# Fifteen products of zeros at the start instead of seven, and two early row loads into another buffer

## The reference

```python
rkv = einsum('blh,hu->blu', inputs, W_rkv) + b_rkv
r, k, v = split(rkv, 3);  r = sigmoid(r);  k = exp(k);  kv = k * v
u1, u2 = scan(y[t] = lam * y[t-1] + (kv, k)[t])
x = (u1 + gamma * kv) / (u2 + gamma * k + 1e-06) * r
x = layernorm(inputs + x @ W_o + b_o)
xr = mu_r * x + (1 - mu_r) * x_prev;  xk = mu_k * x + (1 - mu_k) * x_prev
out = layernorm(x + sigmoid(xr @ W_r.T) * (square(relu(xk @ W_k.T)) @ W_v.T))
```

## Time and profile before

| | before |
|---|---|
| median of 3 runs | 2542.32 us (2540.78 to 2545.28) |
| profiled execution, its own time | 2542.95 us |
| its span (first to last event in the trace) | 2541.2 us |
| PE busy | 2509.6 us, 99% of the span |
| DVE busy | 2099.5 us, 83% |
| ACT busy | 1270.9 us, 50% |
| POOL busy | 1252.2 us, 49% |
| moved by DMA | 110.73 MB |

### The profile page before, as it was taken

One profiled execution on the slowest core, in us unless ns is written; L12 is line 12 of the kernel. 1 busy time (PEld: TensorE's weight loads), 2 busy tenths in 40 slices (PEclk: granted clock), 3 DMA queues, 4 the chain that ended last, 5 costly groups with the idle time before them and its releaser, 6 DMA issues.

```text
span 2541.2 us, 32904 instructions
## 1 busy us (share of the span) xinstructions
PE 2509.6 (99%) x11255; PEld 2075.1 (82%) x11255; DVE 2099.5 (83%) x2693; ACT 1270.9 (50%) x2157; POOL 1252.2 (49%) x1130
## 2 busy tenths in 40 slices
PE   8999999999999999999999999999999999999998
PEld 6788888878888788888888878888888878888877
DVE  8888888878888788887888888888888888888884
ACT  5544455544455354554545544455444555444555
POOL 5744445444454445545455444544444454545544
PEclk9999999999999999999999999999999999999999
DMA  4001101111011110101111111101111111110100
GB/s 178 17 34 50 51 34 36 44 39 51 34 45 39 35 51 34 50 34 35 50 46 38 34 35 50 50 34 34 35 50 50 34 39 31 49 51 34 49 27 34
DMA packets 57791, 110.73 MB, mean 44 GB/s; under 512 B 7041, under 2 KB 7041, under 8 KB 57089
## 3 DMA queue, kind: packets, MB, share of 16 engines
q1 hardware_dynamic: 56736, 108.03, 12.3%
q10 hardware_dynamic: 864, 0.28, 0.1%
HBM read 74.73 MB, written 33.55 MB: 43 GB/s over the span
## 4 chain that ended last, share of the span: by engine, by line
PE 94%; issue 2%; POOL 2%; DVE 1%; ACT 0%; DMA 0%; POOLq 0%; DVEq 0%
PE bankB L1193 13%; PE bankB L1194 13%; PE bankB L1195 13%; PE bankA L1173 13%; PE bankA L1172 13%; PE bankA L1174 13%; PE bankB L1240 4%; PE bankB L1242 4%; PE bankB L1241 4%; PE bankB L1218 2%; POOL xk_lo L449 0%; DVE att_f L939 0%; POOL wk_lo L412 0%; DMA wrkv_f<-in_w_rkv 0%; POOL att_f L422 0%
## 5 line engine op out<-in xcount | busy, mean ns | idle before, releaser
L1173 PE MATMUL bankA<-x_lo,wrkv_hi 128*128 128x512 f32 x1488 | 580.3, 390 | 14.5 <-issue 14.5
L1172 PE MATMUL bankA<-x_hi,wrkv_hi 128*128 128x512 f32 x1488 | 584.3, 393 | 3.5 <-POOL x_lo L417 3.5
L1174 PE MATMUL bankA<-x_hi,wrkv_lo 128*128 128x512 f32 x1488 | 580.4, 390 | 0.0
L923 DVE RECIPROCAL gate<-gate 128x512 f32<-128x512 f32 x128 | 429.2, 3353 | 4.4
L422 POOL TENSOR_TENSOR att_f<-att_f,gate 128x512 f32<-128x512 f32 x128 | 207.1, 1618 | 276.0 <-DVE att_f L944 276.0
L1174 PEld LDWEIGHTS bankA<-x_hi,wrkv_lo 128*128 128x128 f32 x1488 | 280.0, 188 | 74.1 <-issue 15.7
L1172 PEld LDWEIGHTS bankA<-x_hi,wrkv_hi 128*128 128x128 f32 x1488 | 280.2, 188 | 62.3 <-POOL x_lo L417 3.9
L1173 PEld LDWEIGHTS bankA<-x_lo,wrkv_hi 128*128 128x128 f32 x1488 | 280.2, 188 | 57.6 <-issue 0.5
L449 POOL TENSOR_TENSOR xk_lo<-xk_f,xk_hi 128x512 fp32r<-128x512 f32 x124 | 178.8, 1477 | 241.2 <-ACT xk_hi L707 241.2
L699 ACT ACTIVATE z<-z,shift,rstd 128x512 f32<-128x512 f32 x124 | 94.3, 808 | 356.7 <-POOL shift L442 356.7
L920 DVE SCALAR_TENSOR_TENSOR gate<-u,gate 128x512 f32<-128x512 f32 x128 | 182.9, 1429 | 104.2 <-ACT gate L647 101.8
(11 more groups left out here) (160 smaller groups left out, 5607.6 us busy)
## 6 DMA issues: line engine op xcount, KB each, us to landing
y<-in_x SPq DMA_DIRECT2D x128, 256.0 KB, 2.7
x_f<-in_xT SPq DMA_DIRECT2D x124, 256.0 KB, 4.0
out<-z SPq DMA_DIRECT2D x124, 256.0 KB, 2.1
wrkv_f<-in_w_rkv SPq DMA_DIRECT2D x3, 768.0 KB, 9.2
xk_f<-in_xT SPq DMA_DIRECT2D x4, 256.0 KB, 5.6
wo_f<-in_w_o SPq DMA_DIRECT2D x1, 1024.0 KB, 12.4
wr_f<-in_w_r SPq DMA_DIRECT2D x1, 1024.0 KB, 14.9
wv_f<-in_w_v SPq DMA_DIRECT2D x1, 1024.0 KB, 16.7
```

Of the source, the lines that this page charges most:

```text
L923: dve.reciprocal(gate[:, c % 2], gate[:, c % 2]).then_inc(rec_made, 1)
L1172: pe.matmul(bank[:], w_hi, hi[:, h], start=(h == 0), stop=False)
L1173: pe.matmul(bank[:], w_hi, lo[:, h], start=False, stop=False)
L1174: last = pe.matmul(bank[:], w_lo, hi[:, h], start=False, stop=(h == NC - 1))
```

## The change

WARM becomes 15, so `write_columns` issues fifteen products of zeros in place of seven. Block 0's rows for its third and fourth tile are loaded into `t`, in SP's `first_block`, right behind the rows of the first and second tile in `y`, without a wait and with semaphores of their own (`y_first_loaded`). `begin_sum` of block 0 reads them from there. Step 1 has two `load_rows` fewer.

```diff
--- before.py
+++ after.py
@@ -87,7 +87,7 @@
 SLOTS = [(name, first + i) for name, first, n in OTHERS for i in range(n)]
 NBANK = 4
 EXACT = (3,)
-WARM = 7
+WARM = 15
 
 KEY, VALUE, GATE = range(3)
 ORDER = (KEY, GATE, VALUE)
@@ -236,6 +236,7 @@
         x_first = [sem(f"x_first{c}") for c in range(NC)]
         x_loaded = [sem(f"x_loaded{c}") for c in range(NC)]
         y_loaded = [sem(f"y_loaded{i}") for i in range(HT)]
+        y_first_loaded = [sem(f"y_first_loaded{i}") for i in range(HT)]
         stored = [sem(f"stored{i}") for i in range(NT)]
 
         x_hi_made, x_lo_made, x_first_lo = sem("x_hi_made"), sem("x_lo_made"), sem("x_first_lo")
@@ -341,8 +342,12 @@
                 for i in range(HT):
                     tile = HT * half + i
 
-                    wait(sp, sum_begun, s.count(NT, tile - 1))
-                    sp.dma_start(y[:, i], x_rows[s.block() * NT + tile]).then_inc(y_loaded[i], 16)
+                    if not s.first():
+                        sp.wait_ge(sum_begun, s.count(NT, tile - 1))
+                    if s.first() and half:
+                        sp.dma_start(t[:, i], x_rows[tile]).then_inc(y_first_loaded[i], 16)
+                    else:
+                        sp.dma_start(y[:, i], x_rows[s.block() * NT + tile]).then_inc(y_loaded[i], 16)
 
             def load_xT(s):
 
@@ -359,10 +364,12 @@
                 load_weight(W_V)
                 load_weight(W_K)
                 load_rows(s, 0)
+                load_rows(s, 1)
 
             def step(s):
                 s1, s2 = (s.back(1), s.back(2))
-                load_rows(s1, 1)
+                if not s1.first():
+                    load_rows(s1, 1)
                 if s2.exists():
                     store(s2, 1)
                 load_rows(s, 0)
@@ -957,13 +964,17 @@
 
             def begin_sum(s, half):
                 for tile in range(HT * half, HT * half + HT):
-                    dve.wait_ge(y_loaded[tile % HT], s.count(32, 16 * (tile // HT) + 16))
+                    if s.first():
+                        dve.wait_ge((y_loaded, y_first_loaded)[tile // HT][tile % HT], 16)
+                    else:
+                        dve.wait_ge(y_loaded[tile % HT], s.count(32, 16 * (tile // HT)))
                     if s.first() and tile == 0:
                         dve.wait_ge(s_bo, 16)
                     bank_free(dve, s, "WO", tile)
                     if s.first():
                         dve.wait_ge(columns_written, WARM)
-                    dve.tensor_tensor(psum_of(s, "WO", tile)[:], y[:, tile % HT], bo[:], ALU.add).then_inc(sum_begun, 1)
+                    rows = t if s.first() and tile >= HT else y
+                    dve.tensor_tensor(psum_of(s, "WO", tile)[:], rows[:, tile % HT], bo[:], ALU.add).then_inc(sum_begun, 1)
 
             def sum_rows(s, tile):
                 return psum_of(s, "WO", tile)[:]
```

## The result

The changed kernel takes 2523.26 us (median of 6 runs, 2522.33 to 2524.09); the kernel before, timed beside it, 2544.0 us (6 runs, 2540.78 to 2545.56). The ratio is 0.992, 95% interval 0.9907 to 0.9933: 20.7 us less. The profiled execution took 2522.33 us, its span 2520.5 us against 2541.2.

What follows compares the result with a forecast made beforehand. PE's own work (94% of the chain) and the loop turns were taken to bound the kernel; 2542.95 us - 2.2 (early clock) + 0 (loads) = 2540.75, set against the median as 2540.2 us, range 2537.0 to 2543.6 us.

Steps and rivals of the forecast that it cites:

- The first term: Kernel start: fifteen products of zeros raise PE's clock early, so eleven product intervals shrink from 0.427 to 0.227 us, 2.2 us.
- The loads into `t`: DVE's four adds: 0.85 us passes, then is given back by the fourth statistics; taken as 0, bounds -0.85 and +0.7 us.
- The step that failed: PE's six loop-turn waits, 14.5 us, taken as fixed; nothing worth more than the gain in the first 100 us.
- The rival on the turns: PE's loop: eight added products move PE's code, turns get dearer, 2.3 us lost, 2544.6 or 2542.5 us; chance 0.08.
- A term of the range: Behind PE's wait for `x_lo` at 50.84 us: the half-clock stretch varies by 1 us between executions, widening the range.

Runs made afterwards that it cites:

- e1_w15: The kernel before with fifteen products of zeros in place of seven and nothing else: 2523.58 us against 2544.8, ratio 0.9918.
- e2_t_only: The changed kernel with seven products of zeros, so the loads into `t` alone: 2543.97 us against 2544.8, ratio 0.9998.
- e3_pad16: The kernel before with sixteen PE instructions that do nothing behind its seven products of zeros: 2525.42 us, ratio 0.9925.
- e7_drop4: The kernel before without four products of block 0's keys, eight PE instructions fewer ahead of the loop: 2536.75 us, ratio 0.9971.
- e6_pad6: The kernel before with six empty PE instructions behind its seven products of zeros: 2525.27 us, ratio 0.9927.
- e8_drop16: The kernel before without sixteen products of block 0's keys, 32 PE instructions fewer ahead of the loop: 2524.22 us, ratio 0.9923.
- e4_back: The changed kernel without eight products of block 0's keys, so as many instructions ahead of the loop as before: 2539.52 us, ratio 0.9981.
- e5_pad3: The kernel before with three empty PE instructions behind its seven products of zeros: 2546.98 us, ratio 1.0015.

## Why the prediction was wrong

**The first term was right.** "Eleven intervals shrink from 0.427 to 0.227 us, 2.2 us": 2.13 to 2.15 us at every point of the chain named, from ACT's key to the product at 48.71 us. PE's wait for `x_lo` kept its length (3.46 and 3.49 us), and eight products at 0.43 us follow it where seven did. The fifteen products ended at 7.01 us, within the 6.5 to 7.3 us given. The first real product started at 8.10 us, 0.2 us later than before; the prediction had it unmoved. From there to the key it took 3.05 us in place of 5.39 us, 2.3 us less, so two small errors cancel. ACT took the next weights at 11.83 us without a wait for them, near the 11.7 us given.

**The loads into `t` were rightly put at 0**, but not for the reason given. The prediction let DVE win 0.85 us and lose it again at the statistics. DVE won nothing. The adds after the change, then in e1_w15, where the rows still come into `y`:

```profile
53.12 2.39 DVE L977 TENSOR_TENSOR bankB<-y,bo 128x512 f32<-128x512 f32 x2
55.43 3.49 DVE L977 TENSOR_TENSOR bankB<-t,bo 128x512 f32<-128x512 f32 x2
```

```profile
56.36 0.72 DVE L966 TENSOR_TENSOR bankB<-y,bo 128x512 f32<-128x512 f32 x1 [0.99 <-DMA y<-in_x]
57.97 0.82 DVE L966 TENSOR_TENSOR bankB<-y,bo 128x512 f32<-128x512 f32 x1 [0.88 <-DMA y<-in_x]
...
58.71 2.31 DVE L911 TENSOR_TENSOR_SCAN u<-lam,carry,key 128x512 f32<-128x512 f32 x1
```

With the rows there, the third and fourth add take 3.49 us in place of 1.54 us, and the scan behind them starts at 58.83 us against 58.71. The first add had begun 0.13 us later as well (53.12 against 52.99 us). The two loads into `t` landed 15.9 us after their issue at 15.7 and 16.2 us, far ahead of these adds. The waits for the transfers have turned into longer adds: each of the two now starts while POOL is in a subtraction and takes 1.79 and 1.78 us, where an add alone takes 0.7 us. POOL in the changed kernel:

```profile
54.91 1.74 POOL L419 TENSOR_TENSOR wo_lo<-wo_f,wo_hi 128x512 fp32r<-128x512 f32 x1
56.63 1.74 POOL L419 TENSOR_TENSOR wr_lo<-wr_f,wr_hi 128x512 fp32r<-128x512 f32 x1
```

The third add starts at 55.43 us and the fourth at 57.13 us, each 0.5 us behind one of these, and each ends some 0.6 us after it. That the subtractions hold the adds up is read from these places in time; no run tried it by itself.

The 1.0 us between 51 and 100 us looks like a gain of the loads, since e2_t_only has it too. The loads are not needed for it: e3_pad16, which has the rows in `y`, shows it as well. POOL's `rstd` in e1_w15, against DVE's scan of the same moment:

```profile
71.94 1.63 POOL L438 TENSOR_TENSOR rstd<-ve,half_pow 128x2 f32<-128x2 f32 x1
...
71.80 1.26 DVE L939 TENSOR_TENSOR_SCAN att_f<-lam,carry,kv 128x512 f32<-128x512 f32 x1
```

and in e3_pad16:

```profile
74.40 0.70 POOL L438 TENSOR_TENSOR rstd<-ve,half_pow 128x2 f32<-128x2 f32 x1
...
74.47 1.25 DVE L939 TENSOR_TENSOR_SCAN att_f<-lam,carry,kv 128x512 f32<-128x512 f32 x1
```

Where POOL starts 0.07 us ahead of the scan it takes 0.70 us; where it starts 0.14 us behind, 1.63 us. The kernel before had 1.70 us (0.06 us behind), the changed one 0.71 us (0.10 us ahead). Of the twelve traces one more, e7_drop4, has it behind the scan (0.17 us, 1.63 us); in the other nine it starts 0.05 to 0.10 us ahead of the scan or more than a microsecond away from it, and takes 0.70 or 0.71 us. `z`, the transposes and the keys follow from it. From the product behind the wait for `x_lo` to the 192nd behind it, past the keys' waits, PE takes 46.3 us in before and e1_w15, 45.2 to 45.3 us in the changed kernel, e2_t_only and e3_pad16: the same 1.0 us. The two outcomes go with a tenth or two of a microsecond in the order of two engines, which nobody planned, so it counts as luck. One execution of each kernel was traced; whether the order changes between executions of one kernel is not shown.

**The step that failed** stands in the first paragraph of the prediction: "14.5 us in six waits of the kind 'issue' ..., one at each turn of the loop, which no engine ends". The row was read and then taken as a fixed price of a loop, and the next sentence drew the limit from it: "nothing that the change does can be worth more than it gives in the first 100 us". The wait came and went with the count of PE's instructions ahead of the loop, which the change raises by sixteen. The rival on the turns looked at the right place ("The eight products (each with its weight load) move PE's code") and weighed it only as a loss of up to 2.3 us, from the spread between the waits; that the same movement could end the waits altogether, 14.5 us and the half clock behind them, was not asked. The row's other half was there to see: a wait that always stands in front of the same product, L1173, the second of the loop, with no engine as its releaser. The runs showed in its place that the six waits stay with three instructions more ahead of the loop and are gone with six or sixteen more; in the changed kernel that gave 17.4 us at the turns, on top of the 2.2 us that were forecast. Where the waits stay, a transfer of q8 has landed 1.2 to 1.5 us before the product that waits.

What the trace shows of a turn is the size of a transfer of q8 (16,384 bytes), the length of the jump (3.3 to 3.9 us where it is taken, 0.08 us where it is not) and two transfers behind its start. The jump and the first transfer cost nearly nothing, for they run beside products that stand ahead of the loop; the wait ends 1.2 to 1.5 us after the second has landed, 2.4 to 3.3 us into the loop in before and e7_drop4. That the transfers bring PE's code in pieces, and that the end of a piece is what PE waits at, remains the author's reading: with it the author told rightly for each of the runs e1 to e8 whether PE waits at the turns, but no trace shows what is in a transfer.

**A term of the range** was that the second stretch at half clock "varies by 1 us between executions". No run shows it, since one execution of each kernel was traced. Between kernels the stretch behind the wait for `x_lo` did differ: the starts of the products are 0.41 to 0.43 us apart six times in a row in before, seven times in the changed kernel, five times in e1_w15 and thirteen times in e6_pad6 and e8_drop16.

## What to carry to other kernels

A wait "issue" that stands in front of the same instruction at every turn of a loop is worth a trial by itself: add or remove a handful of instructions ahead of the loop, on the engine that sets the time, and time it again. Here six empty instructions gave 18 us of 2543, and the eight products that were added gave 2 us by what they do and 17 as sixteen instructions more. Taking instructions away can end the wait too: 32 fewer did here (e8_drop16), eight fewer made it 0.9 us shorter (e7_drop4). An edit that changes PE's count of instructions ahead of the loop brought or took up to 18 us in these runs, whatever it was meant to do; so compare PE's waits "issue" and the count of instruction transfers before the cause is looked for in the edit.

## What was not expected of the hardware

- At each turn of the loop the trace has two transfers of q8 behind the start of PE's jump. The jump took 3.3 to 3.9 us, beside products issued before it; the second transfer started 0.65 to 1.34 us after its end. In before and e7_drop4 the product that waited started 2.4 to 3.3 us after the loop's first one. Eight instructions fewer ahead of the loop made a wait 0.9 us shorter (1.5 us left of 2.4), 32 fewer ended it (e8_drop16).
- Of the six waits at the turns, one was followed by a stretch at half clock in the kernel before, three in e2_t_only, two in e4_back and two in e5_pad3. Their length does not tell which: those followed by one lasted 2.28 to 3.00 us, the others 2.01 to 3.32 us. The six of e7_drop4, 1.1 to 1.9 us, had none. So such a wait was followed by 1.5 us more or not, and the scatter between runs is larger with the waits (4.8 us over six runs before) than without (1.8 us over six runs after).
- A GpSimd instruction on 128x2 elements (`rstd`) took 0.70 us where it started 0.07 us ahead of a VectorE scan (e3_pad16), and 1.63 us where it started 0.14 us behind one (e1_w15).
